# Two fronts of a graph-attention kernel: penalties, edge lists and moments move to other places

## The reference, cut to what matters

```python
h = x @ W.T                                   # 3750 x (8 heads x 64)
e = leaky_relu(e_src[src] + e_dst[dst], 0.2)  # scores, 60000 x 8
e = e * (1.0 + et_emb[edge_type])             # layer 1 alone
e = e * edge_weight[:, None]                  # layer 1 alone
e = exp(e - max of e over the edges of dst)
alpha = e / (sum of e over the edges of dst)
out = sum over the edges of dst of h[src] * alpha
```

## Time and profile before

| | |
|---|---|
| median of 3 runs | 3353.9 us (3353.35 to 3356.68) |
| the profiled execution | 3356.07 us, its span 3354.4 us |
| granted TensorE clock, mean of the span | 0.916 |
| PE busy | 2836.1 us (85%) |
| DVE busy | 1972.2 us (59%) |
| POOL busy | 1572.1 us (47%) |
| ACT busy | 652.5 us (19%) |

### The profile page before, as it was taken

One profiled execution on the slowest core, in us unless ns is written; L12 is line 12 of the kernel. 1 busy time (PEld: TensorE's weight loads), 2 busy tenths in 40 slices (PEclk: granted clock), 3 DMA queues, 4 the chain that ended last, 5 costly groups with the idle time before them and its releaser, 6 DMA issues. The chain is left out here.

```text
span 3354.4 us, 39519 instructions
## 1 busy us (share of the span) xinstructions
PE 2836.1 (85%) x10120; PEld 1350.1 (40%) x10121; DVE 1972.2 (59%) x3405; ACT 652.5 (19%) x1092; POOL 1572.1 (47%) x1505
## 2 busy tenths in 40 slices
PE   6799888889887871599999579978998888676998
PEld 4344322322224551355554334433222222364765
DVE  6766866666656866523331426677666666666554
ACT  2001300000005640111111110022111111351333
POOL 4572177777760000244443037404777777302655
PEclk9899999999997875699999789999999999757999
DMA  8384477777761221165654666426777777455776
GB/s 260 79 129 144 136 209 209 209 210 209 209 192 56 76 78 55 36 153 144 151 146 117 164 129 118 95 96 185 210 211 211 210 210 210 144 198 150 128 125 106
DMA packets 341665, 512.24 MB, mean 153 GB/s; under 512 B 174474, under 2 KB 179834, under 8 KB 340870
## 3 DMA queue, kind: packets, MB, share of 16 engines
q0 software_dynamic: 115872, 317.04, 37.6%
q1 hardware_dynamic: 96214, 186.03, 17.4%
q10 hardware_dynamic: 129424, 7.21, 2.7%
HBM read 423.42 MB, written 86.70 MB: 152 GB/s over the span
## 5 line engine op out<-in xcount | busy, mean ns | idle before, releaser
L1172 POOL DMA_INDIRECT zg<-z_rows,src_groups x940 | 892.2, 949 | 450.8 <-issue 273.7
L1251 PE MATMUL bank<-zg,aggregate_onehot 128*128 x1888 | 947.6, 629 | 116.7 <-DVE zg L1219 107.7
L1219 DVE TENSOR_TENSOR zg<-zg,bank 128x1024 f32<-128x1024 f32 x470 | 573.8, 1221 | 425.1 <-DMA zg<-z_rows,src_groups 424.7
L1251 PEld LDWEIGHTS bank<-zg,aggregate_onehot 128*128 128x128 f32 x1888 | 306.8, 190 | 755.7 <-issue 750.0
L1885 POOL DMA_INDIRECT exp_xg<-hn_rows,exp_gather_tok x64 | 71.2, 1113 | 503.4 <-DVE exp_gather_tok L1947 380.8
L780 PE MATMUL bank<-alpha,front_table 128*64 128x512 bf16 x2304 | 271.9, 386 | 29.1 <-DVE alpha L646 28.9
L1154 ACT ACTIVATE acc<-bank 128x512 f32<-128x512 f32 x60 | 35.8, 597 | 1080.8 <-PE bank L1251 1080.8
L337 PE MATMUL bank<-zg,x 128*128 128x512 f32 x480 | 220.4, 615 | 17.9 <-ACT front_z L346 11.8
L2029 PE MATMUL bank<-exp_w,exp_h_t 128*117 128x512 f32 x512 | 225.7, 595 | 0.7 <-ACT exp_h_t L1976 0.7
L443 POOL DMA_INDIRECT front_d<-src_scores,src_chunks x192 | 193.4, 1007 | 58.5 <-issue 58.5
L1896 POOL DMA_INDIRECT x_rows<-exp_y,exp_add_tok x64 | 137.2, 2144 | 164.2 <-DVE exp_y L1938 129.0
(11 more groups left out here) (436 smaller groups left out, 3422.0 us busy)
## 6 DMA issues: line engine op xcount, KB each, us to landing
exp_w<-in_L_ffn_w SPq DMA_DIRECT2D x32, 1024.0 KB, 7.4
zg<-src_key SPq DMA_DIRECT2D x64, 384.0 KB, 4.5
zg<-z_rows,src_groups POOLq DMA_INDIRECT x940, 3.7
zg<-src_tile SPq DMA_DIRECT2D x64, 192.0 KB, 3.9
exp_w<-in_L_ffn_W SPq DMA_DIRECT2D x2, 4096.0 KB, 17.4
x_rows<-x SPq DMA_DIRECT2D x10, 768.0 KB, 3.5
hn_rows<-zg SPq DMA_DIRECT2D x10, 768.0 KB, 3.5
x<-x_rows SPq DMA_DIRECT2D x5, 1536.0 KB, 13.6
```

The costliest lines, as they stand in the source:

```text
L1172: pool.indirect_dma_start(zg[:, r, j, :], None, k.z_rows[:, :], bass.IndirectOffsetOnAxis(k.src_groups[:, n:n + 1], 0)).then_inc(gathered[ ...
L1219: v.tensor_tensor(z, z, bcast_last(scales[:, at:at + J * H], DH), ALU.mult).then_inc(msg_ready, 1)
L1251: mm = nc.tensor.matmul(k.banks[:, bass.ds(bank, 1), :].rearrange("p a n -> p (a n)"), onehot_at(n)[:, j, :], zg[:, bass.ds(at, 1), j, :]. ...
```

## The change

The four kinds of penalties of layer 0 are each cut into four parts, and the 16 parts are made in turns 13, 15, ... 43 of the picks. In layer 1 the lists are loaded behind rounds 2, 3 and 4 (six, six and four chunks), the penalties in four loads behind rounds 6 to 9; kinds are found in turn 12, and their products and modify steps go to turns 12 to 20. ACT's wait for mod_read goes to the middle of the picks. In the softmax of layer 1 ACT takes one stretch more before it waits for wide_read, and the stretches have other lengths. In the score part of both layers the moments of group b+1 stand between the fourth and the fifth normalised tile of group b, the root ahead of the sixth copy; `split_sources` follows group 2.

```diff
+PEN_PARTS = 4
+BOUNDS_AT = tuple(range(13, 13 + 2 * 4 * PEN_PARTS, 2))
+LISTS_WITH = {2: range(0, 6), 3: range(6, 12), 4: range(12, CH)}
+BOUNDS_WITH = (6, 7, 8, 9)
+KINDS_AT = 12
-SPREADS_AT = tuple(range(1, 9))
+SPREADS_AT = tuple(range(KINDS_AT, KINDS_AT + 8))
 MODS_AT = tuple(m + 1 for m in SPREADS_AT)
-UNITS_TO = ((10, 33, 47, 69, 83), (9, 37, 51, 76, 90))
+UNITS_TO = ((10, 33, 47, 69, 83), (9, 39, 54, 78, 93))
...
-                for c in range(CH):
+                def load_list(c):
                     rows = slice(c * H, (c + 1) * H)
                     if layer == 0:
                         sp.dma_start(wide[rows, :].bitcast(I32), ...)
                     else:
+                        sp.dma_start(e[rows, :].bitcast(I32), ...)
                         sp.dma_start(wide[rows, 0:CL], ...)
-                        sp.dma_start(e[rows, :].bitcast(I32), ...)
-                if layer == 1:
+
+                if layer == 0:
+                    for c in range(CH):
+                        load_list(c)
+                else:
                     sp.dma_start(et[:, :], I["et_by_kind"]).then_inc(kinds_loaded, 16)
-                    sp.dma_start(bounds, k.run_bounds.rearrange("a p n -> p a n")).then_inc(bounds_loaded, 16)
...
                 for r in range(2, ROUNDS):
                     load_keys(r)
                     load_tiles(r)
+                    if layer == 1:
+                        for c in LISTS_WITH.get(r, ()):
+                            load_list(c)
+                        if r in BOUNDS_WITH:
+                            kind = BOUNDS_WITH.index(r)
+                            sp.dma_start(bounds[:, kind, :], k.run_bounds[kind]).then_inc(bounds_loaded, 16)
...
-                norm(0)
-                stats(1)
-                for b in range(1, NT // SBT):
+                for b in range(NT // SBT):
+                    invert(b)
+                    norm(b, range(HNS))
                     if b + 1 < NT // SBT:
                         stats(b + 1)
-                    if layer == 0 and b == 1:
+                    norm(b, range(HNS, SBT))
+                    if layer == 0 and b == 2:
                         split_sources()
-                    norm(b)
...
+                def make_bounds(step):
+                    which, part = step // PEN_PARTS, step % PEN_PARTS
+                    lo, n = part * (CL // PEN_PARTS), CL // PEN_PARTS
+                    here = dst[:, 1 + lo:1 + lo + n]
+                    if step == 0:
+                        dve.wait_ge(wide_loaded, 16 * CH)
+                        chain(v.tensor_copy(pen[:, 0:2], dst[:, ::CL + 1]))
+                    if which < 2:
+                        v.tensor_scalar(bounds[:, (TO_FIRST, TO_LAST)[which], lo:lo + n], here, pen[:, which:which + 1], -BIG,
+                                        ALU.not_equal, ALU.mult).then_inc(bounds_ready, 1)
+                    else:
+                        other = lo + (0, 2)[which - 2]
+                        out = bounds[:, (PREV, NEXT)[which - 2], lo:lo + n]
+                        chain(v.tensor_tensor(out, dst[:, other:other + n], here, ALU.not_equal))
+                        v.tensor_scalar(out, out, -BIG, None, ALU.mult).then_inc(bounds_ready, 1)
...
                     for t in range(NT):
                         count_inside(t)
-                    make_bounds()
...
                 def between(m):
                     if layer == 1:
+                        if m == KINDS_AT:
+                            find_kinds()
                         if m in MODS_AT:
                             modify(MODS_AT.index(m))
                         return
...
+                    if m in BOUNDS_AT:
+                        make_bounds(BOUNDS_AT.index(m))
...
                 for n in range(NT):
-                    if n % SBT == 3 and n // SBT + 1 < NT // SBT:
+                    if n % SBT == SBT - 1 and n // SBT + 1 < NT // SBT:
                         root(n // SBT + 1)
...
-                if layer == 1:
-                    act.wait_ge(mod_read, MP)
...
                     if m == halfway:
+                        if layer == 1:
+                            act.wait_ge(mod_read, MP)
                         take_sums(0)
...
-                    act.wait_ge(bounds_loaded, 16)
-                    take_upto(projected(0))
+                    act.wait_ge(bounds_loaded, 16 * 4)
+                    take_upto(projected(1))
                     act.wait_ge(wide_read, 1)
```

More of the change, by code:

```diff
@@ L392, in _ @@
                     else:
+                        sp.dma_start(e[rows, :].bitcast(I32), I["type_list"][c * CL:(c + 1) * CL].partition_broadcast(H)).then_inc(kinds_loaded, 16)
                         sp.dma_start(wide[rows, 0:CL], I["weight_list"][c * CL:(c + 1) * CL].partition_broadcast(H)).then_inc(wide_loaded, 16)
-                        sp.dma_start(e[rows, :].bitcast(I32), I["type_list"][c * CL:(c + 1) * CL].partition_broadcast(H)).then_inc(kinds_loaded, 16)
-                if layer == 1:
+                if layer == 0:
+                    for c in range(CH):
+                        load_list(c)
+                else:
                     sp.dma_start(et[:, :], I["et_by_kind"]).then_inc(kinds_loaded, 16)
-                    sp.dma_start(bounds, k.run_bounds.rearrange("a p n -> p a n")).then_inc(bounds_loaded, 16)
                 keys, tiles = (a.rearrange("(c f) -> c f", c=CH) for a in (k.src_key, k.src_tile))
@@ L431, in _ @@
                     load_tiles(r)
+                    if layer == 1:
[4 more added lines that the diff above has]
+                            sp.dma_start(bounds[:, kind, :], k.run_bounds[kind]).then_inc(bounds_loaded, 16)
                 if layer == 0:
-                    sp.wait_ge(bounds_ready, 4)
+                    sp.wait_ge(bounds_ready, 4 * PEN_PARTS)
                     sp.dma_start(k.run_bounds.rearrange("a p n -> p a n"), bounds).then_inc(bounds_stored, 16)
@@ L478, in stats, with invert, norm @@
                     ins.then_inc(var_ready, 1)
-                def norm(b):
+                def invert(b):
                     dve.wait_ge(std_ready, b + 1)
                     chain(v.reciprocal(k.rstd[:, b * SBT:(b + 1) * SBT], std[:, b * SBT:(b + 1) * SBT]))
-                    for j in range(SBT):
+                def norm(b, tiles):
+                    for j in tiles:
                         n = b * SBT + j
@@ L520, in _, with find_kinds @@
                     take_groups()
-                norm(0)
-                stats(1)
-                for b in range(1, NT // SBT):
+                for b in range(NT // SBT):
+                    invert(b)
+                    norm(b, range(HNS))
                     if b + 1 < NT // SBT:
                         stats(b + 1)
-                    if layer == 0 and b == 1:
+                    norm(b, range(HNS, SBT))
+                    if layer == 0 and b == 2:
                         split_sources()
-                    norm(b)
-                if layer == 1:
+                def find_kinds():
                     dve.wait_ge(kinds_loaded, 16 * CH + 16)
@@ L975, in vector @@
                 if layer == 0:
-                    dve.wait_ge(bounds_ready, 4)
+                    dve.wait_ge(bounds_ready, 4 * PEN_PARTS)
                 else:
-                    dve.wait_ge(bounds_loaded, 16)
+                    dve.wait_ge(bounds_loaded, 16 * 4)
                 v.tensor_copy(pen[:, 0:1], bounds[:, TO_FIRST, CL - 1:CL])
@@ L1032, in scalar @@
                 if layer == 0:
-                    act.wait_ge(bounds_ready, 4)
+                    act.wait_ge(bounds_ready, 4 * PEN_PARTS)
                 else:
-                    act.wait_ge(bounds_loaded, 16)
-                    take_upto(projected(0))
+                    act.wait_ge(bounds_loaded, 16 * 4)
+                    take_upto(projected(1))
                     act.wait_ge(wide_read, 1)
```

## The result

The changed kernel takes 3335.0 us (median of 4 runs, 3331.8 to 3342.5) where the kernel before takes 3354.6 beside it: ratio 0.9945 [0.9928, 0.9961], 0.55% faster. Forecast were 3318.0 and 3299 to 3338.

A forecast was written before the change was run, and what follows sets the result against it. It took the two fronts as bound by VectorE's penalties (layer 0), late stores through DMA (layer 1's scores) and TensorE's projections (softmax). 3356.1 - 13.0 - 24.8 + 15 - 13.3 = 3320.0 profiled, 3318 as median; range 3299 to 3338.

The forecast's parts named there:

- Forecast A: Layer 1's picks: the wait for kinds is 6 to 24 us, giving 3309 to 3327; chance 0.47.
- the wait in turn 12: VectorE's DMA wait before layer 1's kinds comparison: about 14 us; under 6 or over 24 makes the prediction wrong.
- Layer 0: Penalties made among the picks, with new moments order and clock: -13.0 us in all, up to F, layer 1's front start.
- the late root: Score part: ScalarE's root moves from fourth to sixth tile, delaying TensorE; layer 0's order of moments taken as +1.2 us.
- The term for the clock (-1.1): Layer 0: TensorE idles some 3 us instead of 16, so its first selections gain 0 to 2.3, taken as 1.1.
- Score part: Layer 1: without lists and penalties, stores land undisturbed, gaps and slow projections go, keys are ready: -24.8 us.
- the wait of 2.77 for VectorE: Layer 1's score part: TensorE's wait for VectorE's long stretch of moments, 2.77 us, removed by the new order.
- The four parts named for the root: Score part: copy 0.58, issue 0.4, root 0.3, reciprocal and first tile 0.7; about 1.6 us once per layer.
- Softmax: Layer 1: VectorE's wait for TensorE shrinks from 12.63 to about 0.7 us; with smaller terms -13.3.
- The same lists among the picks: Layer 1: lists behind rounds 2 to 4 at 1 us each come late for kinds in turn 12: +15 us.
- The upper bound: Layer 1's picks: at 2 us a list, lists end at P + 86.5 (P: first one-hots), costing +43 us.
- rival C: Layer 1's picks: 2 us a list as before, so the wait only moves: +43, 3346 to 3347; chance 0.13.

The follow-up runs named there:

- e7: e2 with all 16 pieces of layer 0's penalties made before the score copies, not between the turns of the picks: 3313.6 us.
- e1: The changed kernel with layer 1's lists loaded as 16 transfers of 16 rows to partitions 8 apart, types first: 3299.0 us.
- e3: The changed kernel with layer 1's old softmax (old stretches, old number of tiles before the wait for wide_read): 3357.5 us.
- e5: The changed kernel with each layer 1 list transfer's 8 rows taken from 8 different stretches and written to partitions 8 apart: 3323.0 us.
- e11: The changed kernel with each list transfer's 8 rows taken from 8 different stretches, still written to 8 neighbouring partitions: 3339.6 us.
- e12: The changed kernel with each list transfer's one stretch, still read 8 times, written to 8 partitions 8 apart: 3322.8 us.
- e2: The changed kernel with layer 1's 32 list loads back ahead of the keys; penalties stay behind rounds 6 to 9: 3298.1 us.
- e8: e2 with the old order of moments in layer 0 alone and layer 0's lists issued behind its first keys: 3303.5 us.
- e6: e2 with the one 3840 KB load of the penalties back ahead of the keys in the score part: 3317.4 us.
- e9: e6 with the old order of moments in both layers: 3319.1 us.

## Why the prediction was right, and where it was off

The median of 3335.0 lies in the range of 3299 to 3338, and in part by luck. Forecast A had 3309 to 3327, and the prediction called itself wrong if the wait in turn 12 is over 24 us; it was 29.98. The stages of the profiled execution were to give 36.1 us and gave 13.6, and its 3342.49 lies outside the range. The median came inside because the four executions differ by 10.7 us, and because 6.7 us came unforecast from the softmax and from behind it.

**Layer 0, right.** The work left the path: score copies at 92.17 ("about 91"), one-hots at 95.5 ("94 to 96"), pieces free, the late root there, and e7 gives 15.5 back in the median. At F the forecast was -13.0 and -13.8 was measured, but that closeness is chance: the changed kernel, e1, e3, e5, e11 and e12 have the same code up to F, and F lies at 1862.0 to 1870.3. The term for the clock (-1.1) did not come: the first selections take 8.30 us after a gap of 3, not less than after 16.

**Score part, right in size, half right in cause.** -24.8 against -23.7, stores at 2.0, no gap over 3. But the gaps were laid to "the 32 list loads and the penalties" as one thing. e2 has them apart: with lists there and penalties gone, one-hots are 1.2 us later (5.6 in e8). The prediction therefore let the lists' move stand as the price of this gain, and it wasn't. Of the small terms, the wait of 2.77 for VectorE was to go and is there, 2.78 at 1896.43; the wait of 3.25 for ScalarE before it went instead, so that the first projection comes 2.9 earlier after F (3.2 forecast). The four parts named for the root add up to 1.98 and not 1.6; 1.76 and 1.81 were measured.

**Softmax, right.** -13.3 against -15.6; e3 gives 15.5. The second carry waits 0.32, as forecast nearly nothing, and the sum's carry behind it 1.17 where it waited 2.89.

**The step that failed** is the rate in "The same lists among the picks": "Light traffic is the nearer case: 32 lists at 1 us", +15. Measured were 2 us a list for most of the time and +43.9. The upper bound had it to the place: "2 us a list gives P + 86.5, +43", and the kinds' wait ended at P + 86.25. That is the mechanism and the size of rival C, given 0.13. C's sum would be 3348 for a profiled execution; 3342.5 came, as the softmax gave 2.3 more and what lies behind it 4.4. The words for the two rates, other traffic or none, were not wrong, but the traffic that counts was overlooked: the keys and tiles that the change itself puts between the lists, on the same queue. Beside them the lists came at 2 us, and alone at 1.3 to 1.7 (24 to 19 packets in 4 us), never at the 1 us of 66 to 70 us. And the prediction did not ask what a list's eight rows write to, which sets how much that traffic costs (e11 against e12). What made the window of 66 to 70 us fast was not tried.

**A wait not foreseen:** 14.59 us for keys in turn 9. The prediction wrote that "each load of later keys and tiles is queued behind them", and asked only when the lists would be there. It seems to have changed the place of the loss more than its sum, since what is waited for there is the same queue; no run parts the two.

The Trainium skill's page "SBUF — State Buffer" (Door 1: The DMA port swizzle) says that DMA bandwidth depends on how many of 16 ports the partitions reach, 27.2 GB/s each. By its table of ports, partitions 0 to 7 reach two, eight partitions 8 apart in one half four, all sixteen eight. That is an estimate of 54, 109 and 218 GB/s from the page's figures; packets of 15360 bytes give 61 (16 in 4 us, after), 108 (28, e12) and 215 (56, e1). The trace agrees in these stretches. It does not agree throughout: lists to neighbours alone on the queue came at 22 packets in 4 us, 84 GB/s (after, 2024 to 2028), and in e2 at up to 29, 111 GB/s, above what two ports would give, with lists of several chunks under way. So the ports fit where the difference arose, and are not shown to be its cause. The page cited in the prediction, "DMA: Bandwidth & Descriptors" (the rule on how many engines a copy uses stands in its section Why a DMA increments its semaphore by 16 and not by 1), by which a transfer of eight rows uses eight engines, would not make e12 and e11 differ; for e5 against e1 it gives the same factor of two as the ports do, and no run parts them.

**Not a gain of the change:** the 4.4 us behind the first message. The code there is the same in all fourteen kernels, and the profiled executions take 1043.3 to 1047.8 us for it, 1047.7 before and 1043.3 after.

**Open:** why the order of moments costs 9.4 us beside late stores and 1.2 without them, and why the medians of e6 and e9 don't show it; why the wait for lists differs by 8 us between executions; why traffic on the queue slows rows to neighbours more.

## What to carry to other kernels

Before a group of transfers moves, take away one of its members at a time: here a single load of 3840 KB cost 10.8 us, and 32 small ones, which cost a few at most, were moved with it, to a place where they cost 44 us. A rate read from two windows is a range, not a choice; if the bound decides 28 us of the sum, ask which property of the transfer sets it, and what else will lie in its queue. Spreading the rows of a small transfer over the partitions, 8 apart, was worth 12 to 17 us in the median (e5 and e12 against after and e11). Sixteen rows at a time, with what is needed first issued first, was worth 24 more (e1 against e5).

## What the runs showed of the hardware

- Rows of 15 KB on SP's queue, counted in the first stretches of 4 us: to 8 neighbouring partitions 13 to 19 packets, some 2 us for a list of 120 KB; to 8 partitions 8 apart 21 to 30, 1.1 to 1.5 us; to 16 partitions 8 apart 33 and 56. Whether the rows come from one stretch of memory or from eight makes no difference (13 to 17 and 16 to 19; 21 to 29 and 24 to 30).
- The same rows to neighbours, with nothing else on the queue, came at 19 to 24 packets (after); 8 apart at 23 to 27 (e12).
- PE's first selections took 7.83 us after 16.48 us of idle time (before) and 8.30 after 3.01 (after), both in layer 0: the shorter gap did not shorten them.
- With the new order of moments, stores of z that landed in 2.0, 12.4, 13.5, 13.8 and 15.7 us (after, e2, e7, e8, e6) went with 0.9, 1.9, 1.5, 4.4 and 4.2 us of PE's waiting for late copies behind the first projection: of ten to fourteen microseconds of lateness, less than four reached PE.
